# Attention value products: one lump of 256 query columns behind every pair of scores instead of one of 512 behind every second pair

## The reference

```python
x = L0_attn_x
x = x + 0.5 * _L0_ffn_ref(_layernorm(x, axis=-1), L0_ffn_gate_w, L0_ffn_Wg, L0_ffn_Wu, L0_ffn_Wd)
x = x + _L0_attn_ref(_layernorm(x, axis=-1), ...)
x = x + 0.5 * _L0_ffn_ref(_layernorm(x, axis=-1), L0_ffn_gate_w, L0_ffn_Wg, L0_ffn_Wu, L0_ffn_Wd)

# in _L0_attn_ref: 16 heads of width 8, 512 queries and 512 keys
aperture = jax.nn.sigmoid(x @ Wa + ba)
expression = jax.nn.sigmoid(x @ We + be)
alignment = jnp.einsum('bhqd,bhkd->bhqk', inner, outer) / scale
attn_align = jax.nn.softmax(alignment, axis=-1)
attn = attn_align * aperture.transpose(0, 2, 1)[..., :, None] * expression.transpose(0, 2, 1)[..., None, :]
attn = attn / (attn.sum(axis=-1, keepdims=True) + 1e-08)
converged = jnp.einsum('bhqk,bhkd->bhqd', attn, v)
```

## Time and profile before

| What | Value |
|---|---|
| device time, median of 3 runs | 474.01 us (473.26 to 474.25) |
| the profiled execution | 472.87 us |
| its span in the profile | 471.1 us |
| PE, DVE, ACT, POOL busy | 400.4, 382.7, 233.9, 56.2 us |
| first scores of step 0 to first scores of step 15 | 163.2 to 338.3 us |
| steps 2 to 13 | 188.5 to 326.9 us |

### The profile page before, as it was taken

One profiled execution on the slowest core, in us unless ns is written; L12 is line 12 of the kernel. 1 busy time (PEld: TensorE's weight loads), 2 busy tenths in 40 slices (PEclk: granted clock), 3 DMA queues, 4 the chain that ended last, 5 costly groups with the idle time before them and its releaser, 6 DMA issues.

```text
span 471.1 us, 7748 instructions
## 1 busy us (share of the span) xinstructions
PE 400.4 (85%) x2220; PEld 214.9 (46%) x2220; DVE 382.7 (81%) x875; ACT 233.9 (50%) x441; POOL 56.2 (12%) x105
## 2 busy tenths in 40 slices
PE   3606999999888999999999999999988049999995
PEld 2503456776453543333333333333436015567764
DVE  6598967789889888988999899987545889767883
ACT  3400443342532167777777777778873005343322
POOL 2720002212000210000000000000004600021210
PEclk9999999999897579999999999999997559999999
DMA  6200011223077811111111111100200000112103
GB/s 169 59 0 1 0 35 38 65 67 89 28 276 233 324 36 46 53 52 51 47 51 53 52 44 52 45 1 3 68 1 0 0 1 1 35 33 67 44 24 90
DMA packets 25768, 27.49 MB, mean 58 GB/s; under 512 B 3920, under 2 KB 17488, under 8 KB 25680
## 3 DMA queue, kind: packets, MB, share of 16 engines
q1 hardware_dynamic: 25744, 27.20, 18.7%
HBM read 17.08 MB, written 9.98 MB: 57 GB/s over the span
## 4 chain that ended last, share of the span: by engine, by line
PE 79%; DVE 13%; ACT 4%; issue 2%; DMA 1%; DVEq 0%; ACTq 0%
PE ps L1211 14%; PE ps L1221 13%; PE ps L1196 7%; PE ps L1040 6%; PE ps L1078 6%; PE ps L1061 3%; PE ps L1063 3%; PE ps L1062 3%; DVE heads_out L739 3%; PE ps L1093 3%; PE ps L1094 3%; DVE values L736 3%; ACT probs L630 2%; PE ps L1003 2%; DVE neg_max L849 2%
## 5 line engine op out<-in xcount | busy, mean ns | idle before, releaser
L849 DVE TENSOR_REDUCE neg_max<-ps 128x1 f32<-128x512 f32 x256 | 160.8, 680 | 14.0 <-PE ps L1196 13.9
L630 ACT ACTIVATE probs<-ps 128x512 f32<-128x512 f32 x256 | 137.2, 602 | 42.4 <-PE ps L1211 41.2
L1196 PE MATMUL ps<-stacks 63*128 63x512 f32 x256 | 106.3, 498 | 1.5 <-DVE neg_max L849 1.1
L1211 PE MATMUL ps<-stacks 64*128 64x512 f32 x256 | 94.9, 461 | 4.7 <-ACT probs L630 4.6
L1211 PEld LDWEIGHTS ps<-stacks 64*128 64x128 f32 x256 | 41.1, 188 | 75.8 <-ACT probs L630 65.1
L1221 PE MATMUL ps<-probs,v_ext 128*32 128x512 f32 x512 | 69.0, 612 | 0.0
L1196 PEld LDWEIGHTS ps<-stacks 63*128 63x128 f32 x256 | 43.9, 196 | 18.2 <-DVE neg_max L849 13.9
L540 ACT CAST stacks<-ps 128x512 fp32r<-128x512 f32 x32 | 17.2, 590 | 66.9 <-PE ps L1040 66.9
L779 DVE TENSOR_TENSOR probs<-slot_row,slot 128x512 f16<-128x512 f16 x64 | 39.2, 686 | 0.1
L459 POOL TENSOR_TENSOR w_lo<-w_gu,w_hi 128x512 fp32r<-128x512 f32 x16 | 20.3, 1276 | 143.1 <-ACT w_hi L525 143.1
L804 DVE TENSOR_TENSOR vae_and_gates<-heads_out,ps 128x512 f32<-128x512 f32 x32 | 21.7, 687 | 16.9 <-ACT heads_out L548 9.0
(11 more groups left out here) (157 smaller groups left out, 531.8 us busy)
## 6 DMA issues: line engine op xcount, KB each, us to landing
stacks<-parts_dram SPq DMA_DIRECT2D x64, 128.0 KB, 2.4
parts_dram<-part_hi SPq DMA_DIRECT2D x8, 512.0 KB, 3.5
parts_dram<-part_lo SPq DMA_DIRECT2D x8, 512.0 KB, 5.2
w_gu<-in_L_ffn_Wg_dram SPq DMA_DIRECT2D x16, 128.0 KB, 2.1
w_gu<-in_L_ffn_Wu_dram SPq DMA_DIRECT2D x16, 128.0 KB, 2.2
wd_sb<-in_L_ffn_Wd_dram SPq DMA_DIRECT2D x16, 128.0 KB, 2.2
x<-in_L_attn_x_dram SPq DMA_DIRECT2D x4, 256.0 KB, 3.5
stacks<-k_rows_dram SPq DMA_DIRECT2D x2, 512.0 KB, 6.8
```

The lines of the kernel that those rows point to most:

```text
L630: nc.scalar.activation(probs[:, u // HG, u % HG, :], ps[:, RING + ring_bank(step, u), :], ACT.Exp, scale=SCORE_SCALE).then_inc(probs_ready, 1)
L849: nc.vector.tensor_reduce(neg_max[:, g, col, qt:qt + 1], ps[:, ring_bank(step, u), :], AX.X, ALU.max, negate=True).then_inc(max_taken, 1)
L1196: nc.tensor.matmul(ps[:, ring_bank(step, u), :], q_stack[rows, g, pp, chunk(qt)], k_stack[rows, g, pp, :], start=True, stop=True).then_inc ...
L1211: nc.tensor.matmul(ps[:, RING + ring_bank(step, u), :], k_stack[rows, g, pp, chunk(c)], q_stack[rows, g, pp, :], start=True, stop=True).th ...
```

## The change

The lump of 512 columns becomes two of 256 for chunks 1, 2 and 3; chunk 0 keeps its 512 columns. Each half has its own four weight loads and matmuls. `PRODUCTS_AT` says what stands behind which pair: pair 0 has the second half of chunk 2 of the step before, pairs 1 and 2 the halves of chunk 3 of it, pair 3 nothing, pair 4 all of chunk 0, pairs 5 and 6 the halves of chunk 1, pair 7 the first half of chunk 2. The copy of heads goes to behind exponential 5, `turn_heads` to behind pair 5, and the normalization to behind reduction 11 (by count). `probs_used` is counted up by the second half only. Behind the last step stand half a lump and a whole one.

```diff
-        HEADS_AT, TURN_AT = 3, 4
-        NORM_AT = 9
+        HEADS_AT, TURN_AT = 5, 5
+        NORM_AT = 11
+        BOTH = (0, 1)
+        PRODUCTS_AT = {0: (-2, (1,)), 1: (-1, (0,)), 2: (-1, (1,)), 4: (0, BOTH), 5: (1, (0,)), 6: (1, (1,)), 7: (2, (0,))}
...
-            def products(n, g, c):
+            def products(n, g, c, halves=BOTH):
...
+                queries = slice(S // 2 * halves[0], S // 2 * (halves[-1] + 1))
                 for j in range(HG):
-                    last = nc.tensor.matmul(ps[32 * j:32 * j + 32, 6, :], v_ext[:, g, c, j, :], probs[:, c, j, :],
-                                            start=(c == 0), stop=(c == C - 1))
-                last.then_inc(probs_used, 1)
+                    last = nc.tensor.matmul(ps[32 * j:32 * j + 32, 6, queries], v_ext[:, g, c, j, :], probs[:, c, j, queries],
+                                            start=(c == 0), stop=(c == C - 1), skip_group_check=True)
+                if halves[-1] == 1:
+                    last.then_inc(probs_used, 1)
...
-                    if k == 1 and not first:
-                        products(n - 1, (g - 1) % G, C - 1)
-                    if k in (3, 5, 7):
-                        products(n, g, k // 2 - 1)
+                    if k in PRODUCTS_AT:
+                        c, halves = PRODUCTS_AT[k]
+                        if c >= 0:
+                            products(n, g, c, halves)
+                        elif not first:
+                            products(n - 1, (g - 1) % G, C + c, halves)
                     if not first and k == TURN_AT:
                         turn_heads(n - 1, g - 1, n + (2 if has_next else 1))
...
+            products(B * G - 1, G - 1, C - 2, (1,))
             products(B * G - 1, G - 1, C - 1)
```

## The result

| What | Before | After |
|---|---|---|
| device time, median of the runs | 473.63 us (472.86 to 474.25) | 483.22 us (482.72 to 483.96) |
| ratio | | 1.0211 (95% interval 1.0194 to 1.0228) |
| profiled execution, and its span | 472.87, 471.1 us | 483.96, 482.2 us |
| steps 2 to 13 of the attention | 138.38 us | 144.70 us |
| an ordinary step | 11.47 us | 11.92 us |

The change costs 9.6 us, where +7.2 was forecast. The predicted 481.2 (474.9 to 486.8) had the sign and the range, and was 2.0 short. The two profiled executions lie 11.1 apart, more than the medians; 10.0 of it is in the attention's 16 steps (6.3 in steps 2 to 13, 2.1 in step 14, 1.2 in step 15, 0.4 in steps 0 and 1), the other 1.1 in stages that the change doesn't touch. Behind the last scores the halves were to cost nothing, and did: the copy of the heads starts 2.95 behind the last scores, where it was 2.93.

The account below looks back on a forecast made before the run. Neither PE nor DVE was full; a ring of 2.77 us per lump bound the kernel. The terms 4.1 + 2.3 + 1.4 - 0.6 = +7.2 on 472.87 gave 480.1, or 481.2 on the median, range 474.9 to 486.8.

Parts of the forecast that it names:

- The price of a half lump: PE's value products: a half lump takes 0.57 us, 1.14 for two, against 1.00 for a whole lump.
- the fixed 0.14: Part of a lump on PE, 0.14 us for changing shape of tile and back, that halving leaves whole.
- The ring through the normalization: Steps 2 to 13: new ring through DVE and PE, 11.75 a step, 11.87 by the longer way through ACT.
- the idle time at `den_a`: Sign on DVE at the first normalizing operation: 0.7 to 1.0 idle behind the heads' transposes, where it was 0.21.
- The sum of steps 2 to 13: Twelve attention steps at 11.87 instead of 11.53: +4.1 us.
- the turn of the loop: Loop's branch, 0.3 in each fourth step, falls ahead of the wait for reduction 15 and may vanish.
- At nothing: Terms put at no cost: POOL's refill, ACT's writing, SP's maxima row, and the loop's branch, -0.9 at most.
- Steps 14 and 15: Last two attention steps: +2.3 and +1.4 us, from halves on PE, later transpose of the maxima and waits for exponentials.
- Steps 0 and 1: First attention steps: lumps come a pair later, nearer the rise of the clock, -0.6 us (bounds 0 and -1.2).
- Smoother work wins: Rival: the ring through the normalization doesn't close, only PE's need of 10.58 a step counts; 465 us, chance 0.11.
- Halves are free: Rival: half lumps at 0.43 each, steps of 11.45; 474 to 476 us (0.50 each gives 478), chance 0.09.
- Halves are dearer: Rival: half lumps at 0.68 each, +0.33 a step over the forecast; 486 us, chance 0.09.

Follow-up runs that it names:

- experiment 3: Kernel before with lumps of chunks 1, 2 and 3 cut into halves back to back where the whole lump stood: 473.20 us, ratio 0.9998.
- Experiment 1: Changed kernel with the normalization behind 12 reductions instead of 11: 478.23 us, ratio 1.0096.
- experiment 5: Changed kernel with the transposes of the heads behind pair 4 and the normalization behind 10 reductions: 477.24 us, ratio 1.0081.
- 4: Kernel before, whole lumps in place, with only the moved copy (exponential 5), transposes (pair 5) and normalization (11 reductions): 490.24 us, ratio 1.0345.
- Experiment 6: Changed kernel with another order of PSUM banks at the hardware loop's turn, the body's last unit in another bank: 482.00 us, ratio 1.0187.
- experiment 2: Kernel before with the normalization behind 10 reductions instead of 9: 471.31 us, ratio 0.9946.
- Experiment 9: As experiment 8, but chunk 0's sum opened once, and whole lumps, copy and transposes of before in steps 14 and 15: 469.85 us, ratio 0.9917.
- experiment 11: Kernel before, whole lumps behind pairs 1, 3, 6, 7, transposes behind pair 5, normalization behind 13, other bank order at the loop's turn: 469.39 us, ratio 0.9907.
- experiment 8: Changed kernel with chunk 0 halved too, copy behind exponential 4, transposes behind pair 3, normalization behind 8 reductions: 472.61 us, ratio 0.9980.

## Why the prediction was right, and where it was short

**The price of a half lump**: 0.57 worked out, 0.57 measured. That the fixed 0.14 belongs to the visit and stays whole with each half was argued then and is shown now by experiment 3. That it is the change of shape of tile, and not that of number type, stays argued. The visits go from four to seven a step; the prediction's "doubles" was too much.

**The ring through the normalization**: 11.87 a step worked out, 11.92 measured, `den_a` idle 0.87 worked out, 0.78 measured. Experiment 1 takes one reduction out of the ring, experiment 5 a pair and a half lump; either alone gives 11.5 to 11.6, and 4 shows the moves alone to be dear. So of the 0.45 an ordinary step, 0.35 to 0.40 goes with the ring and can be had back without touching a half. The prediction named the idle time at `den_a` as the sign of the ring; experiment 5 shows that it proves nothing: nearly the same idle time in a shorter step.

**The sum of steps 2 to 13** is the step that failed: +4.1 forecast, +6.3 measured. 0.6 of the difference is 0.05 a step. The rest is the turn of the loop, a term put at nothing: I took it for the branch, at 0.3, and let it vanish ahead of reduction 15's wait. The sum had even taken it off already, since it sets 11.87 without a turn against 11.53, which is an average with the turns in it, so that the "-0.9 at most" under *At nothing* was in the forecast. Experiment 6 shows that it is for the most part no branch but a wait for banks: the steps around the three turns are over 11.92 by 1.7 in all, where the kernel before was over 11.47 by 0.7. Why it grew stays open. It is not the ring through the normalization, for where that is eased it is no smaller: 1.9 in experiment 1, and 1.3 in experiment 2.

**Steps 14 and 15**: +2.3 and +1.4 forecast, +2.1 and +1.2 measured. The size held; of one part the reason isn't shown. I put 0.85 a step down to the copy of the heads behind a delayed half lump. In step 14 of the changed kernel:

```profile
338.98 0.64 PE L1224 MATMUL ps<-probs,v_ext 128*32 128x256 f32 x8
339.55 0.73 PE L1213 MATMUL ps<-stacks 64*128 64x512 f32 x3
...
339.69 0.59 ACT L624 COPY heads_out<-ps 128x512 f32<-128x512 f32 x1 [0.70 <-PE ps L1224]
340.17 2.07 ACT L632 ACTIVATE probs<-ps 128x512 f32<-128x512 f32 x4
...
340.82 0.49 PE L1213 MATMUL ps<-stacks 64*128 64x512 f32 x1 [0.55 <-ACT probs L632]
```

The copy does stand there, and scores 9 (340.82) wait for exponential 6 (340.17), as worked out. But scores 6 themselves come only at 339.55, behind the half lump, and an exponential starts 0.61 behind its scores: exponential 6 would start at 340.16 without the copy too, and with no lump behind pair 3 nothing hides the wait. No experiment separates the two.

**Steps 0 and 1**: -0.6 forecast, with bounds of 0 and -1.2, +0.4 measured, outside them. Step 0 is 13.37 instead of 13.52, no clear gain, since in the kernels of experiments 1, 5 and 6, which leave that step all but as the change has it, it takes 13.23 to 13.63. Step 1 went from 11.78 to 12.30. The ring closes in it as well (`den_a` idle 0.78): 0.45 of its 0.52 is what every ordinary step lost, and the sum, which counted the ring from step 2 on, had left it out.

**The rivals.** *Smoother work wins*: not in this kernel. Experiment 9 gives 3.6 us with halves behind every pair, experiment 11 4.0 with whole lumps, so that a gain is there to be had and the halves are not what it takes. It decided where I had put it, at the place of `den_a`. *Halves are free* and *Halves are dearer*: the trace's 0.57 excludes 0.43, 0.50 and 0.68.

## What to carry to other kernels

When work is moved along one engine's fixed order, follow each ring that closes through the moved step, around to its own start in the next round, and add it up; the longest one sets the step, and neither busy shares nor an idle gap names it. Count every wait in the code on that way, those that end early now and those at a loop's turn. Before cutting a group of matmuls smaller, see what stands around it: here each visit paid its fixed 0.14 us again, however small the group was. And try the one number that places the waiting operation before building anything: here it gave nearly half of the loss back, and half a per cent to the kernel before.

## What the runs showed of the hardware

A visit of four fp32 matmuls on 32-column strips, between fp32r matmuls on half the rows, costs about 0.14 us beyond its streaming, an estimate from the starts (0.57 for half the columns, 1.00 for all, 1.00 for two halves in one visit). Within a visit, sixteen fp32 passes of 256 columns take what eight of 512 take, 1.00 against 0.99 in experiment 3, in spite of their weight loads. And a sum opened by one matmul in half of a bank's columns did not leave the other half's sum alone: with the start flag on both halves (experiment 8) the output is off by 0.17 (relative), with it on the first half alone (experiment 9) both halves are summed. That it was chunk 0's share of the first half that was lost is inferred from the order of the two. The Trainium skill, "PSUM — Partial Sum Buffer", The four PSUM rules, says that such a flag clears the marks that decide between adding and overwriting over the whole bank, whichever of its columns are written; this agrees.
